# First-layer biases of the expert units applied by ScalarE from columns, low parts formed on GpSimd

## The chip, the cores and the metric

The kernel runs on one core of a Trainium2 chip. The metric is the device time of one execution in microseconds (us). TensorE multiplies, VectorE and ScalarE work on tiles in SBUF and in the matmul accumulator (PSUM), GpSimd works on SBUF, and SyncE issues most DMAs. Each engine runs its own list of instructions in order and waits on semaphores for the others.

## What the reference computes

The input x is 16 batches of 128 tokens with 256 features. Four stages are added to it in turn:

```
x = x + attention(layernorm(x), ctx, mask)              # one masked attention
x = x + experts(layernorm(x))                           # 2 of 4 encoder layers for each batch
x = x + causal_attention(layernorm(x), ctx)             # 16 heads
x = x + shared_ffn_and_top1_of_8(layernorm(x))

# one encoder layer (expert e):
x1 = layernorm(x + attention_16_heads(x)) * n1w + n1b
ff = relu(x1 @ l1w.T + l1b) @ l2w.T + l2b               # 256 -> 1024 -> 256
out = layernorm(x1 + ff) * n2w + n2b
```

The change touches `l1b`, the biases of the first layer inside `relu`, in the second stage.

## The kernel before

A **unit** is one batch with one of its two chosen experts: 32 units, one batch being units 2b and 2b+1. The stage is written as a fully unrolled list of blocks, n = -1 to 32, and each engine has its own function `block` that gives its order within a block. Block n works on four units at once: unit m = n+1 gets its scores, unit n its attention values and output projection, unit f = n-1 its first layer norm and hidden layer, unit g = n-2 its second layer, and unit n-3 its second layer norm. In even blocks the next batch is also prepared (`kp` is not None there): normalised tokens are transposed and split. In odd blocks its statistics are taken. Blocks 31 and 32 do this too for the causal stage that follows.

Every float32 product is made from bf16 parts: a high part and a low part (value minus high part), with three matmuls per product.

What the order is on each engine in block n (names are the functions of the kernel, lines are those of the profile):

- **TensorE**: `projection_v(m)`; `second(g,1)`; `values(n)` (L716); `x1_transposes(f)` (L492, reads x1, waits for `x1_ready(f)`); `second(g,0)`; `o_rows(n)`; `scores(m)`; in even blocks `prep`; `hidden(f,1)` (L752 to L756); `o_transposes(n)`; `hidden(f,0)`; `shift_transpose(m)` (L679, waits for VectorE's maxima of the scores); `out_proj(n)` (L498 to L500, waits for VectorE's `o_low(n)`); `projection_qk` of the next unit (L632 to L642, waits for `yT_ready`, which `y_low` gives in even blocks); `scores_T(m)`.
- **ScalarE**: `exps(n)`, `qk_hi(m)`, `o_evict(n)`, `x1_hi(f)`, in even blocks `prep`, `relu(f,1)` (L1149), `oo(n)`, `shift(m)`, `relu(f,0)`.
- **VectorE**: `norm1(f)`, `bias_v(m)`, `add_expert(n-4)`, in even blocks `y_of`, then `qk_low(m)`, `x1_low(f)`, `sum2(g)`, `o_norm(n)`, `maxima(m)`, `shift_split(m)`, `o_low(n)` (L1542), `norm2(n-3)` (L1288, waits for GpSimd's root `l2_rstd`), in even blocks `y_low` (L1502), `h_low(f,1)` (L1569), `sum1(n)` and its statistics, `h_low(f,0)`, statistics of g, in odd blocks statistics of the next batch.
- **GpSimd**: `rstd(1)` for unit f (L1980, L1982), in even blocks `y_root`, `y_bias(m)` (L2054), `affine1(f)` (L2064, L2066, which gives `x1_ready(f)`), `x1_bias(f)` (L2073), `rstd(2)` for unit n-3, `affine2(n-3)` (L2077, L2079, waits for `norm2(n-3)`).

In `hidden` each of the eight 128-column slices of the hidden layer starts with a product of the bias row (split into high and low rows in `b1hl`) with a row selector, and then takes six weight products. `relu` reads PSUM once (128x512) and writes the high part `hh`; `h_low` reads PSUM again and writes the low part `hl`. `second` multiplies both with the second layer's weights.

Of the kernel before, what the change touches and what calls it, by code (L numbers as in the profile page):

```python
# [80 lines left out]
B_QK = DFF  # L81
B_ALL = DFF + 2 * D
# [43 lines left out]
def encoder_kernel(nc, x_d, ctx_d, mask_d, maskt_d, w_d, wc_d, vec_d, vc_d, b1_d, gw_d, gb_d, sw_d, sv_d, tw_d, tvec_d, tg_d, tb_d,  # L126
# [8 lines left out]
    with stack:  # L135
# [10 lines left out]
        b1hl = sb("b1hl", [128, B_ALL], bf16)  # L146
        cst = sb("cst", [128, C_ALL])
# [57 lines left out]
        kraw = vec[:, 0:K_ALL]  # L205
        gl = h[:, 0:12 * B * E].rearrange("p (k j) -> p k j", j=B * E)
# [27 lines left out]
        def sem(name):  # L234
# [18 lines left out]
                                    "gveps", "grstd", "g", "gm", "gmean"))  # L253
        mask_ready, neg_ready, g_sums, g_centred = a_m01, a_neg, a_sm, a_sn
# [72 lines left out]
        def head(g, c, s):  # L327
            return 8 * c + 2 * g + s

        b1f = [(0, 512, v[0:NROW, :, :].rearrange("p h k -> p (h k)")), (512, 512, qk[0:NROW, :]),  # L330
               (B_QK, D, khm[0:NROW, :, :, :].rearrange("p c s k -> p (c s k)").bitcast(f32)),
# [23 lines left out]
        def _(sp):  # L355
# [16 lines left out]
            for c0, width, rows_f in b1f:  # L372
                sp.dma_start(rows_f, b1_d[:, c0:c0 + width]).then_inc(b1_in, 16)
            sp.dma_start(s12_raw, sw_d[:, 0:KC * 2 * HM]).then_inc(sw_in, 16)
# [111 lines left out]
        def _(pe):  # L486
# [253 lines left out]
            def hidden(u, half, base, e):  # L740

                if half == 1:
                    pe.wait_ge(x1T_split, u + 1)
                elif not isinstance(u, int) or u > 0:
                    pe.wait_ge(res2, u)

                def w(t, c, j):
                    return t[:, ds(base + (W_L1 + 512 * half + 128 * j + c * DFF), 128)]
                for j in range(4):
                    b0 = 512 * half + 128 * j  # L750
                    dst = ps[:, 7 - half, 128 * j:128 * j + 128]
                    mm(dst, b1hl[:, b0:b0 + 128], row_of(e), start=True, stop=False)  # L752
                    for c in range(KC):
                        mm(dst, w(w_hi, c, j), xh[:, c, :], start=False, stop=False)  # L754
                        mm(dst, w(w_hi, c, j), xl[:, c, :], start=False, stop=False)  # L755
                        last = mm(dst, w(w_lo, c, j), xh[:, c, :], start=False, stop=(c == KC - 1))  # L756
                last.then_inc(h_b if half else h_a, 1)

            def second(u, half, base):

                if half == 1:
                    pe.wait_ge(hl_b, u + 1)
                    pe.wait_ge(hl_a, u + 1)
# [161 lines left out]
            pe.wait_ge(b1_ready, 4)  # L925
# [102 lines left out]
        def _(act):  # L1028
# [47 lines left out]
            for i in range(PAIRS):  # L1076
# [14 lines left out]
                if i == 2:  # L1091
                    act.wait_ge(b1_zero, 1)
                    act.wait_ge(b1_in, 16 * 4)
# [53 lines left out]
            def relu(u, half):  # L1147
                act.wait_ge(h_b if half else h_a, u + 1)
                A(hh[:, 4 * half:4 * half + 4, :], ps[:, 7 - half, :].rearrange("p (c k) -> p c k", k=128),  # L1149
                  ACT.Relu).then_inc(hh_b if half else hh_a, 1)  # L1150

            def block(n, kp):
# [9 lines left out]
                if kp is not None:  # L1162
                    prep(kp, 2 * KC if isinstance(kp, int) and kp >= B else KC)
                if encodes(f):
                    relu(f, 1)
                if attends(n):
                    oo(n)
# [107 lines left out]
        def _(dve):  # L1275
# [106 lines left out]
            for i in range(PAIRS):  # L1382
# [11 lines left out]
                if i + 2 < PAIRS:  # L1394
                    if i == 0:
                        dve.wait_ge(x_third, 16)
                    if i == 1:
                        dve.wait_ge(x_in2, 16)
# [8 lines left out]
                if i == 4:  # L1407
                    dve.wait_ge(b1_ready, 4)
# [158 lines left out]
            def h_low(u, half):  # L1567
                dve.wait_ge(hh_b if half else hh_a, u + 1)
                stt(hl[:, 4 * half:4 * half + 4, :], ps[:, 7 - half, :].rearrange("p (c k) -> p c k", k=128), 0.0,  # L1569
                    hh[:, 4 * half:4 * half + 4, :], ALU.max, ALU.subtract).then_inc(hl_b if half else hl_a, 1)  # L1570

# [88 lines left out]
            def block(n, slot, bias_m, add_b, ks, kp):  # L1660
# [28 lines left out]
                if encodes(f):  # L1689
                    h_low(f, 1)  # L1690
# [6 lines left out]
                if encodes(f):  # L1697
                    h_low(f, 0)
# [128 lines left out]
            dve.wait_ge(sv_in, 32)  # L1827
            for b in range(1, B):
# [145 lines left out]
        def _(pool):  # L1974
# [92 lines left out]

            def x1_bias(u, slot, base):
# [12 lines left out]
            def block(n, slot, ex, kp, km):  # L2081

                m, f = n + 1, n - 1
                if encodes(f):
                    rstd(1, n, l1_var, l1_veps, l1_rstd)
                if kp is not None:
# [30 lines left out]
            def block_c(b, slot, ex=None, weights=False, tokens=False):  # L2117
                n = b + UNITS
                if served(b - 1):
                    rstd(1, b + (A1 - 1), s_var, s_veps, s_rstd)  # L2120
                if served(b + 1):
# [28 lines left out]
            def base_of(u):  # L2150
                return digit(words_pool[u // WORD], u % WORD) * V_EXP
            for n in range(-1, UNITS + 1):
# [132 lines left out]
```

## Time and profile before

| what | value |
|---|---|
| median of 3 runs | 782.21 us (781.33 to 782.88) |
| the profiled execution's own time | 782.31 us |
| its span, first to last instruction | 780.5 us |
| TensorE busy | 716.6 us (92%) |
| VectorE busy | 620.0 us (79%) |
| GpSimd busy | 378.5 us (48%) |
| ScalarE busy | 338.8 us (43%) |
| mean granted TensorE clock | 0.962 of full speed |

Busy time is an average over stages with different limits: the expert units run from about 100 us to 550 us of the span. TensorE's clock has two levels, 2.4 GHz (1.00) and 1.2 GHz (0.50). A row of the timeline gives the start, the duration, the engine, the line, what is written from what, and in brackets how long the engine had been idle and what ended the wait. A row of a stretch gives its length and the busy time and instructions of TensorE's matmuls, its weight loads, VectorE, ScalarE and GpSimd, then the mean granted clock, the DMA share and GB/s.

### The profile page before, as it was taken

What the parts mean: (1) busy time and instruction counts of PE and PEld (TensorE: products, weight loads), DVE (VectorE), ACT (ScalarE), POOL (GpSimd) and SP (SyncE); (2) the same over time, 40 slices, a digit from 0 to 9 for tenths busy, and PEclk for the clock granted to TensorE, in tenths of its full rate; (3) what the DMA queues carried; (4) which work ended last, traced back from release to release, by engine and by line L of the source; (5) the groups of instructions that cost most, each with busy time, mean ns of one, the idle gap of its engine ahead of it and who ended that gap; (6) DMA issues with size and microseconds to landing.
All of it is one profiled execution on the core that took longest, in us unless ns stands there. A gap on an engine that the chain in (4) does not pass through costs nothing.

```text
span 780.5 us, 29149 instructions
## 1 busy us (share of the span) xinstructions
PE 716.6 (92%) x11014; PEld 567.3 (73%) x11014; DVE 620.0 (79%) x1803; ACT 338.8 (43%) x711; POOL 378.5 (48%) x637
## 2 busy tenths in 40 slices
PE   5687879999999999999999999999999999987896
PEld 4466557888888888888888888888666566665684
DVE  4686665878888878888797878788889988997864
ACT  4676224343434344343434343434455555553210
POOL 4688523353535354544545353534434554547354
PEclk9797689999999999999999999999999999999798
DMA  9787200000000000000000000000112232322120
GB/s 313 253 266 274 89 2 3 3 3 3 3 3 4 3 3 3 3 3 3 3 3 4 3 3 3 3 16 10 43 57 81 78 90 90 104 89 69 38 73 7
DMA packets 24799, 40.98 MB, mean 53 GB/s; under 512 B 3871, under 2 KB 16809, under 8 KB 24411
## 3 DMA queue, kind: packets, MB, share of 16 engines
q1 hardware_dynamic: 23240, 37.13, 14.3%
q8 instruction: 96, 1.57, 0.8%
q0 software_dynamic: 704, 1.71, 0.8%
q10 hardware_dynamic: 726, 0.30, 0.2%
q14 instruction: 33, 0.27, 0.1%
HBM read 30.60 MB, written 8.91 MB: 51 GB/s over the span
## 4 chain that ended last, share of the span: by engine, by line
PE 69%; DVE 13%; POOL 5%; issue 4%; DMA 4%; ACT 4%; POOLq 0%; SPq 0%; ACTq 0%; DVEq 0%
PE ps L498 7%; PE ps L492 7%; PE ps L500 6%; PE ps L499 6%; PE ps L698 6%; DVE mx L1522 4%; PE ps L640 4%; PE ps L716 4%; PE ps L754 4%; PE ps L756 3%; PE ps L755 3%; DMA stage<-in_w 3%; PE ps L642 3%; PE ps L641 2%; PE ps L752 2%
## 5 line engine op out<-in xcount | busy, mean ns | idle before, releaser
L1131 ACT ACTIVATE pT<-ps 128x1024 f32<-128x1024 f32 x96 | 93.1, 1021 | 123.2 <-PE ps L698 123.2
L1522 DVE TENSOR_REDUCE mx<-ps 128x16 f32<-128x2048 f32 x48 | 109.5, 2281 | 1.0 <-PE ps L659 1.0
L2077 POOL TENSOR_TENSOR y<-y,vec 128x256 f32<-128x256 f32 x32 | 23.2, 726 | 171.3 <-DVE y L1288 171.3
L754 PE MATMUL ps<-xh,w_hi 128*128 128x128 bf16 x512 | 99.4, 219 | 0.0
L755 PE MATMUL ps<-xl,w_hi 128*128 128x128 bf16 x512 | 99.3, 219 | 0.0
L756 PE MATMUL ps<-xh,w_lo 128*128 128x128 bf16 x512 | 99.3, 219 | 0.0
L1982 POOL TENSOR_TENSOR rs<-rs,cst 128x1 f32<-128x1 f32 x132 | 75.6, 573 | 10.3
L1980 POOL TENSOR_TENSOR rs<-mv,cst 128x1 f32<-128x1 f32 x132 | 28.0, 212 | 99.7 <-DVE mv L1285 93.1
L498 PE MATMUL ps<-w_hi,hh 128*128 x256 | 69.8, 273 | 0.0
L499 PE MATMUL ps<-w_hi,hl 128*128 x256 | 69.8, 273 | 0.0
L500 PE MATMUL ps<-w_lo,hh 128*128 x256 | 69.8, 273 | 0.0
L1149 ACT ACTIVATE hh<-ps 128x512 bf16<-128x512 f32 x64 | 38.4, 600 | 67.8 <-PE ps L756 67.8
L640 PE MATMUL ps<-ycT_hi,w_hi 128*128 128x128 bf16 x256 | 58.9, 230 | 0.2
L641 PE MATMUL ps<-ycT_lo,w_hi 128*128 128x128 bf16 x256 | 56.8, 222 | 0.0
L642 PE MATMUL ps<-ycT_hi,w_lo 128*128 128x128 bf16 x256 | 56.7, 222 | 0.0
L752 PE MATMUL ps<-kst,b1hl 128*128 x256 | 56.2, 220 | 0.1
L754 PEld LDWEIGHTS ps<-xh,w_hi 128*128 x512 | 50.1, 98 | 1.2 <-issue 0.2
L2014 POOL TENSOR_TENSOR w_lo<-stage,w_hi 128x384 bf16<-128x384 f32 x48 | 45.4, 978 | 10.9 <-ACT w_hi L1032 10.9
L755 PEld LDWEIGHTS ps<-xl,w_hi 128*128 x512 | 50.1, 98 | 0.0
L756 PEld LDWEIGHTS ps<-xh,w_lo 128*128 x512 | 50.1, 98 | 0.0
L632 PE MATMUL ps<-kst,b1hl 128*128 (+1 forms) x192 | 42.7, 222 | 1.8 <-issue 0.6
L698 PE MATMUL ps<-qh,khm 32*128 32x128 bf16 x768 | 43.6, 217 | 0.4 <-ACT mT L1032 0.4
(361 smaller groups left out, 2436.1 us busy)
## 6 DMA issues: line engine op xcount, KB each, us to landing
stage<-in_w SPq DMA_DIRECT2D x32, 384.0 KB, 4.9
vec<-in_vec SPq DMA_DIRECT2D x4, 896.0 KB, 5.7
vec<-in_tw SPq DMA_DIRECT2D x12, 256.0 KB, 2.9
ctxc<-in_ctx SPq DMA_DIRECT2D x19, 128.0 KB, 2.2
comb<-x SPq DMA_DIRECT2D x16, 128.0 KB, 1.7
comb<-x1b SPq DMA_DIRECT2D x16, 128.0 KB
out<-x SPq DMA_DIRECT2D x16, 128.0 KB, 2.1
ytok<-t SPq DMA_DIRECT2D x14, 128.0 KB, 1.8
```

Source lines behind the costliest of these rows:

```text
L498: mm(dst, lhs_hi(j), rhs_hi(j), start=(first and j == 0), stop=False)
L499: mm(dst, lhs_lo(j), rhs_hi(j), start=False, stop=False)
L500: last = mm(dst, lhs_hi(j), rhs_lo(j), start=False, stop=(final and j == chunks - 1))
L640: mm(dst, w1, ycT_hi[:, src, :], start=False, stop=False)
L642: last = mm(dst, w2, ycT_hi[:, src, :], start=False, stop=(c == KC - 1))
L698: last = mm(att[:, g, 2 * c + s, :], lhs, rhs, start=(not causal and k == 0), stop=stop)
L754: mm(dst, w(w_hi, c, j), xh[:, c, :], start=False, stop=False)
L755: mm(dst, w(w_hi, c, j), xl[:, c, :], start=False, stop=False)
L756: last = mm(dst, w(w_lo, c, j), xh[:, c, :], start=False, stop=(c == KC - 1))
L1131: A(pT[:, 8 * a:8 * a + 8, :].rearrange("p h q -> p (h q)"), ps[:, 2 * a:2 * a + 2, :].rearrange("p g k -> p (g k)"), ACT.Exp, scale=SCALE ...
L1522: nc.vector.tensor_reduce(mx[:, :], att.rearrange("p g s k -> p (g s) k"), AX.X, ALU.max, negate=True).then_inc(m_max, 1)
L1982: tt(rs[:, i, :], rs[:, i, :], halves, ALU.pow).then_inc(done, 1)
```

## The change

The bias of the first layer is no longer multiplied in by TensorE. It is loaded as columns (`bcols`), eight columns for each expert; GpSimd copies a unit's eight columns into a ring of four slots (`bunit`), and ScalarE's `relu` adds a column to each 128-column slice. A column differs between slices, so `relu` is now four activations for each half, which write float32 (`hf`), and one more copy that makes the high part `hh` from it. The low part is `hf` minus `hh`; both lie in SBUF, and GpSimd computes it instead of VectorE. On GpSimd `h_low(n-2,0)` stands behind the first root of the block, and `h_low(f,1)` behind `x1_bias(f)` and ahead of `rstd(2)` and `affine2(n-3)`. On ScalarE `oo(n)` now stands ahead of `relu(f,1)`. The start of the kernel loads and splits two bias row pieces instead of four.

```diff
@@ TensorE, hidden
-                    b0 = 512 * half + 128 * j
                     dst = ps[:, 7 - half, 128 * j:128 * j + 128]
-                    mm(dst, b1hl[:, b0:b0 + 128], row_of(e), start=True, stop=False)
                     for c in range(KC):
-                        mm(dst, w(w_hi, c, j), xh[:, c, :], start=False, stop=False)
+                        mm(dst, w(w_hi, c, j), xh[:, c, :], start=(c == 0), stop=False)
@@ TensorE, second
                 if half == 1:
                     pe.wait_ge(hl_b, u + 1)
+                    pe.wait_ge(hh_a, u + 1)
+                else:
                     pe.wait_ge(hl_a, u + 1)
@@ ScalarE
             def relu(u, half):
                 act.wait_ge(h_b if half else h_a, u + 1)
-                A(hh[:, 4 * half:4 * half + 4, :], ps[:, 7 - half, :].rearrange("p (c k) -> p c k", k=128),
-                  ACT.Relu).then_inc(hh_b if half else hh_a, 1)
+                act.wait_ge(bunit_ready, 1 + u + 1)
+                if u > 0:
+                    act.wait_ge(hl_b if half else hl_a, u)
+                for j in range(4):
+                    k = 4 * half + j
+                    last = A(hf[half][:, 128 * j:128 * j + 128], ps[:, 7 - half, 128 * j:128 * j + 128], ACT.Relu,
+                             bias=bunit[:, u % RING, k:k + 1])
+                last.then_inc(hf_ready, 1)
+                act.wait_ge(hf_ready, 16 + u * 2 + (1 if half else 2))
+                copy(hh[:, 4 * half:4 * half + 4, :], hf[half].rearrange("p (c k) -> p c k", k=128)).then_inc(hh_b if half else hh_a, 1)
@@ ScalarE, block
+                if attends(n):
+                    oo(n)
                 if encodes(f):
                     relu(f, 1)
-                if attends(n):
-                    oo(n)
@@ VectorE, block
-                if encodes(f):
-                    h_low(f, 1)
...
-                if encodes(f):
-                    h_low(f, 0)
@@ GpSimd
+            def h_low(u, half):
+                pool.wait_ge(hh_b if half else hh_a, u + 1)
+                tt(hl[:, 4 * half:4 * half + 4, :], hf[half].rearrange("p (c k) -> p c k", k=128),
+                   hh[:, 4 * half:4 * half + 4, :], ALU.subtract).then_inc(hl_b if half else hl_a, 1)
+
+            def unit_bias(u):
+
+                cols = bcols[:, ds(digit(words_pool[u // WORD], u % WORD) * B_COLS, B_COLS)]
+                nc.gpsimd.tensor_copy(bunit[:, u % RING, :], cols).then_inc(bunit_ready, 1)
@@ GpSimd, block
                 if encodes(f):
                     rstd(1, n, l1_var, l1_veps, l1_rstd)
+                if encodes(n - 2):
+                    h_low(n - 2, 0)
                 if kp is not None:
                     y_root(kp)
...
                 if encodes(f):
                     affine1(f, ex(-1))
                     x1_bias(f, 1 - slot, ex(-1))
+                if encodes(f):
+                    h_low(f, 1)
                 if encodes(n - 3):
                     rstd(2, n - 2, l2_var, l2_veps, l2_rstd)
                     affine2(n - 3, ex(-3))
+                if encodes(n + 2):
+                    unit_bias(n + 2)
@@ SyncE, at the start
+            sp.dma_start(bcols[:, :], bc_d).then_inc(bcols_in, 16)
```

## Rows read from the trace of the kernel before

**Rows 1.** The page, part 1: busy time, share of the span, instructions.

```profile
PE 716.6 (92%) x11014; PEld 567.3 (73%) x11014; DVE 620.0 (79%) x1803; ACT 338.8 (43%) x711; POOL 378.5 (48%) x637
```

**Rows 2.** Timeline of TensorE in the units.

```profile
300.79 0.23 PE L632 MATMUL ps<-kst,b1hl 128*128 x1
...
307.09 0.33 PE L492 MATMUL ps<-cst,x 128*128 128x128 f32 x1
...
312.85 0.22 PE L756 MATMUL ps<-xh,w_lo 128*128 128x128 bf16 x1
312.90 0.22 PE L679 MATMUL ps<-identb,mtile 128*128 128x128 bf16 x1
...
313.19 0.28 PE L498 MATMUL ps<-w_hi,ooh 128*128 x1
...
320.32 0.41 PE L492 MATMUL ps<-cst,x 128*128 128x128 f32 x2
```

**Rows 3.** Timeline of VectorE in the units.

```profile
299.71 0.40 DVE L1288 TENSOR_SCALAR y<-t,mv,rs 128x256 f32<-128x256 f32 x1
300.03 0.42 DVE L1502 TENSOR_TENSOR ycT_lo<-ps,ycT_hi 128x256 bf16<-128x256 f32 x1
...
312.64 0.42 DVE L1542 TENSOR_TENSOR ool<-ps,ooh 128x256 bf16<-128x256 f32 x1
```

**Rows 4.** Timeline of ScalarE: first half's relu in three blocks (even, odd, even).

```profile
298.32 0.60 ACT L1149 ACTIVATE hh<-ps 128x512 bf16<-128x512 f32 x1 [1.19 <-PE ps L756]
...
311.31 0.60 ACT L1149 ACTIVATE hh<-ps 128x512 bf16<-128x512 f32 x1 [3.22 <-PE ps L756]
...
324.78 0.60 ACT L1149 ACTIVATE hh<-ps 128x512 bf16<-128x512 f32 x1 [1.19 <-PE ps L756]
```

**Rows 5.** Timeline of GpSimd, from odd block to even block.

```profile
313.56 0.73 POOL L2077 TENSOR_TENSOR y<-y,vec 128x256 f32<-128x256 f32 x1 [6.25 <-DVE y L1288]
314.46 0.73 POOL L2079 TENSOR_TENSOR y<-y,vec 128x256 f32<-128x256 f32 x1 [0.18 <-POOL y L2077]
315.25 0.19 POOL L1980 TENSOR_TENSOR rs<-mv,cst 128x1 f32<-128x1 f32 x1
315.52 0.55 POOL L1982 TENSOR_TENSOR rs<-rs,cst 128x1 f32<-128x1 f32 x1
316.96 0.31 POOL L1980 TENSOR_TENSOR rs<-mv,cst 128x1 f32<-128x1 f32 x1 [0.89 <-DVE mv L1285]
...
317.86 0.72 POOL L2054 TENSOR_TENSOR ybo<-y,vec 128x256 f32<-128x256 f32 x1
318.54 0.73 POOL L2064 TENSOR_TENSOR x<-x,vec 128x256 f32<-128x256 f32 x1
319.44 0.73 POOL L2066 TENSOR_TENSOR x<-x,vec 128x256 f32<-128x256 f32 x1 [0.17 <-POOL x L2064]
```

**Rows 6.** Groups by line: shapes, count, busy us and mean ns, idle before.

```profile
L752 PE MATMUL ps<-kst,b1hl 128*128 x256 | 56.2, 220 | 0.1
L1569 DVE SCALAR_TENSOR_TENSOR hl<-ps,hh 128x512 bf16<-128x512 f32 x64 | 42.9, 671 | 0.0
L2101 POOL TENSOR_TENSOR w_lo<-vec,w_hi 128x512 bf16<-128x512 f32 x12 | 13.9, 1161 | 0.0
L1056 ACT ACTIVATE t<-ps,mx 128x128 f32<-128x128 f32 x8 | 2.9, 362 | 0.0
L1032 ACT CAST vec<-vec 128x512 bf16<-128x512 f32 x1 | 0.6, 602 | 0.0
```

**Rows 7.** Groups by line, forms apart: a bias row piece at the start.

```profile
L1032 ACT CAST b1hl<-v 5x512 bf16<-5x512 f32 x1 | 0.6, 612 | 0.0
```

**Rows 8.** Timeline of TensorE; two stretches: busy times, then granted clock, DMA.

```profile
111.95 0.29 PE L679 MATMUL ps<-identb,mtile 128*128 128x128 bf16 x1 [2.25 <-DVE mtile L1530]
...
111.00:117.00 6.00, 4.92 (x47) 4.17 (x51) 3.33 (x11) 0.27 (x1) 1.53 (x4) 0.50 0.01 3
...
770.00:773.00 3.00, 3.00 (x15) 1.92 (x14) 1.07 (x3) 0.00 (x0) 0.99 (x1) 0.53 0.02 5
```

More of the change, by code:

```diff
@@ L80 @@
 K_ALL = K_ROW + NROW
-B_QK = DFF
-B_ALL = DFF + 2 * D
+B_QK = 0
+B_ALL = 2 * D
+B_COLS = FC
+RING = 4
 def batch_of(u):
@@ L123, in served, with encoder_kernel @@
     return not isinstance(b, int) or 0 <= b < B
-def encoder_kernel(nc, x_d, ctx_d, mask_d, maskt_d, w_d, wc_d, vec_d, vc_d, b1_d, gw_d, gb_d, sw_d, sv_d, tw_d, tvec_d, tg_d, tb_d,
+def encoder_kernel(nc, x_d, ctx_d, mask_d, maskt_d, w_d, wc_d, vec_d, vc_d, b1_d, bc_d, gw_d, gb_d, sw_d, sv_d, tw_d, tvec_d, tg_d, tb_d,
                    ib_d, it_d, cst_d, kst_d, pos_d, out, comb_d, ytok_d, keys_d):
@@ L146, in encoder_kernel @@
         b1hl = sb("b1hl", [128, B_ALL], bf16)
+        bcols = sb("bcols", [128, E * B_COLS])
+        bunit = sb("bunit", [128, RING, B_COLS])
+        hf_a = sb("hf_a", [128, 512])
         cst = sb("cst", [128, C_ALL])
@@ L205, in encoder_kernel @@
         kraw = vec[:, 0:K_ALL]
+        hf = (hf_a, h[:, 512:1024])
         gl = h[:, 0:12 * B * E].rearrange("p (k j) -> p k j", j=B * E)
@@ L253, in encoder_kernel @@
                                     "gveps", "grstd", "g", "gm", "gmean"))
+        bcols_in, hf_ready, bunit_ready = x_in2, x_in1, b1_zero
         mask_ready, neg_ready, g_sums, g_centred = a_m01, a_neg, a_sm, a_sn
@@ L328, in head @@
             return 8 * c + 2 * g + s
-        b1f = [(0, 512, v[0:NROW, :, :].rearrange("p h k -> p (h k)")), (512, 512, qk[0:NROW, :]),
-               (B_QK, D, khm[0:NROW, :, :, :].rearrange("p c s k -> p (c s k)").bitcast(f32)),
+        b1f = [(B_QK, D, khm[0:NROW, :, :, :].rearrange("p c s k -> p (c s k)").bitcast(f32)),
                (B_QK + D, D, klm[0:NROW, :, :, :].rearrange("p c s k -> p (c s k)").bitcast(f32))]
@@ L924, in _ @@
             pe.wait_ge(w_hi_ready, PAIRS * 4)
-            pe.wait_ge(b1_ready, 4)
+            pe.wait_ge(b1_ready, 2)
             pe.wait_ge(vones_ready, 4)
@@ L1092, in _ @@
                     act.wait_ge(b1_zero, 1)
-                    act.wait_ge(b1_in, 16 * 4)
+                    act.wait_ge(b1_in, 16 * 2)
                     for c0, width, rows_f in b1f:
@@ L1397, in _ @@
                     if i == 1:
-                        dve.wait_ge(x_in2, 16)
+                        dve.wait_ge(x_in2, 32)
                     pair_stats(i + 2)
@@ L1407, in _ @@
                 if i == 4:
-                    dve.wait_ge(b1_ready, 4)
+                    dve.wait_ge(b1_ready, 2)
                     for slot in range(2):
@@ L1565, in x1_low @@
                    ALU.subtract).then_inc(x1T_split, 1)
[L1567 to L1570, printed above, removed]
             def sum2(u, slot):
@@ L1827, in _ @@
             dve.wait_ge(sv_in, 32)
+            dve.wait_ge(hl_b, UNITS)
             for b in range(1, B):
@@ L2120, in block_c @@
                     rstd(1, b + (A1 - 1), s_var, s_veps, s_rstd)
+                if b == 1:
+                    h_low(UNITS - 1, 0)
                 if served(b + 1):
@@ L2151, in base_of @@
                 return digit(words_pool[u // WORD], u % WORD) * V_EXP
+            pool.wait_ge(bcols_in, 32)
+            unit_bias(0)
             for n in range(-1, UNITS + 1):
@@ L2253 @@
     vc = cat([at["bv"], at["bo"], f1["s_ln_g"], f1["s_ln_b"]])[None, :]
-    b1 = cat([cat([f0["lin1_b"], f0["in_proj_b"][:, :2 * D]], axis=1),
-              cat([np.zeros(DFF, np.float32), at["bq"], at["bk"]])[None, :]])
+    b1 = cat([f0["in_proj_b"][:, :2 * D], cat([at["bq"], at["bk"]])[None, :]])
+    bc = f0["lin1_b"].reshape(E * B_COLS, 128).T
     e12 = cat([cat([f1["ew1"][e], f1["ew2"][e]]).T for e in range(EM)], axis=1)
@@ L2268 @@
         "maskt": a["mask_Bx1xS2_ik1"].reshape(B, S).T,
-        "w": w, "wc": wc, "vec": vec, "vc": vc, "b1": b1,
+        "w": w, "wc": wc, "vec": vec, "vc": vc, "b1": b1, "bc": bc,
         "gw": f0["gate_w"].T.reshape(KC, 128, E).transpose(1, 0, 2), "gb": f0["gate_b"][None, :],
```

## The prediction

> **What bounds the kernel now.** I read the page first: TensorE is busy 92% of the span, VectorE 79%, GpSimd 48%, ScalarE 43% [rows 1]. Next the timeline of the units, engine by engine, since there the change acts. The reader is to see in the TensorE rows that matmuls follow each other at 0.05 to 0.06 us, and that the next wait is already near: the transpose of the maxima starts at 312.90, but out_proj only at 313.19 [rows 2], because VectorE's o_low runs from 312.64 to 313.06 [rows 3]. Last the GpSimd rows, which show a chain that ends almost on TensorE's path. norm2 comes in at 313.56, then follow affine2, the root of unit f, y_root, y_bias and affine1, which ends at 320.17 [rows 5]; x1_transposes starts at 320.32 [rows 2], 0.15 later. In the odd-to-even step GpSimd has nothing to spare. GpSimd idles 6.25 us before affine2 [rows 5], but its place in the order matters, not its load.
>
> One block lasts 12.99 us (298.32 to 311.31, even to odd) or 13.47 us (311.31 to 324.78, odd to even) [rows 4]; 26.5 us a pair.
>
> **The change part by part.**
>
> TensorE: 8 matmuls a unit go, 256 in all [rows 6], at a pitch of 0.056 us: 0.45 us a unit, 14.3 us in all. They stand in hidden, beside VectorE's chain of maxima, split and o_low. Removing 0.45 us there brings TensorE earlier to out_proj, where in the odd block it already waits for VectorE. So even alone this part would yield little. What I use below is 0.22 us for the half that ends before relu(f,1).
>
> ScalarE: relu(f,1) was one operation of 0.60 us [rows 4]. A bias from a column at 128 elements is not there for relu; the nearest row is an exp with such a bias, 0.362 us [rows 6], overlapping the next by 0.10, as other ScalarE rows do: 3 x 0.26 + 0.36 = 1.14 us. Bounds: 0.60 (the pieces cost what one did) and 1.45 (no overlap). I take 1.14, the same form. Then 0.1 for waiting for its own result, and the copy, 0.60 [rows 6]. The Trainium skill, "ScalarE: Activation LUTs", section "What ACT_TABLE_LOAD costs", gives 280 ns plus 0.833 ns an element with a pointer bias and 93 ns of overlap: by it, as an estimate, four pieces take 1.27 us instead of 1.14. The row is used. The copy reads SBUF and its row has the same shape. The added waits of relu, for the unit's columns and for the low part of the unit before, are met early: unit_bias runs two blocks ahead, and the low parts are done a block before (their price if not: relu would move by the lateness, one for one). ScalarE itself has cover: it idled 3.22 us before relu in the odd block [rows 4]. The second half's extra 1.2 us lies ahead of the next exps, where projection_qk and scores_T (3.3 us of TensorE) cover it. shift(m) now stands behind a longer relu(f,1), but its result is only needed after projection_qk, 2.2 us later.
>
> VectorE: both h_low go, 2 x 0.67 us a unit [rows 6]. That brings the root of the next unit and the batch statistics up to 1.3 us forward: 0.89 us of GpSimd's idle time before y_root [rows 5] could go, the largest gain that I see in it. But VectorE first has to get past norm2, see below.
>
> GpSimd: two h_low a unit. The same form, two inputs of 128x512 into bf16, takes 1.16 us [rows 6]. Bounds: 0.73 (one of 256 columns) and 1.46 (twice that) [rows 5]. I take 1.16. The Trainium skill, "GPSIMD Engine Reference", section "Engine selection", says that two-input elementwise work belongs on VectorE and is about 2x slower on GpSimd; the rows give 1.16 against 0.67, 1.7x. By the page, an estimate of 2 x 0.67 = 1.34, each block would be 0.36 longer than in the sum below. unit_bias copies 8 columns: between 0.19 (one column) and 0.73 (256) [rows 5]; I take 0.25.
>
> The step that decides is the new place. On GpSimd h_low(f,1) waits for ScalarE's high part of this block, and behind it are queued rstd(2) and affine2 of unit n-3, then the next block's root, h_low(.,0), y_root, y_bias and affine1. On VectorE norm2(n-3) waits for rstd(2), and behind norm2 are queued y_low, sum1, all statistics, norm1 and bias_v. I add it up from T, the moment ScalarE sees the end of hidden(f,1):
>
> - oo first, to 0.5; four pieces to 1.66; own result and copy to 2.36
> - GpSimd h_low from 2.46 to 3.62; rstd(2), 0.82 [rows 5], to 4.4
> - 0.17 to VectorE; norm2, 0.40 [rows 3], from 4.6 to 5.0 (before it ran right behind o_low)
> - 0.19 to GpSimd; affine2, 1.63 (313.56 to 315.19) [rows 5], to 6.8; unit_bias to 7.05
> - root of unit n 0.82 to 7.85; h_low(.,0) 1.16 to 9.0; y_root 0.90 to 9.9; y_bias 0.68 to 10.6; affine1 1.63 to 12.2; x1_transposes at 12.35.
>
> From x1_transposes to the next T TensorE works without a stop: 320.32 to 324.78 is 4.46, less 0.22 is 4.24 [rows 2, 4]. Odd to even is then 12.35 + 4.24 = 16.6 us, before 13.47: +3.1. TensorE would be ready for x1_transposes near 8.7 (320.2 - 311.3 - 0.22) and stands 3.5 us.
>
> Even to odd there is no y_root: 11.45. But y_low follows norm2, from 4.92 to 5.34, and projection_qk waits for it until 5.45 (before, 300.79 - 298.32 = 2.5); from there to x1_transposes it took 6.30 (300.79 to 307.09) [rows 2]. So 11.75, plus 4.22 - 0.22 = 4.0, is 15.75, before 12.99: +2.75.
>
> A pair gains some 5.8 us. The whole chain needs norm2, so it holds from block 3 to 32: 29 steps x 2.9 = 84 us. The same delay shows once more where the causal blocks take over, +3. At the start two of four bias pieces go, 0.61 us on ScalarE each with overlap [rows 7], and as much on VectorE beside it: -1. The new load of 16 KB takes the place of two small ones and costs nothing; if it did, statistics of the later batches would wait for it. Sum: +86 on the profiled execution's 782.3, which is 0.1 from the median: 868 us.
>
> **The clock.** At 111.95 TensorE came out of a wait of 2.25 us, and over 111 to 117 us the granted clock was 0.50 (1.2 GHz) [rows 8]. The 4.92 us busy there [rows 8] would have been some 2.5 us at 2.4 GHz. Each pair now has a wait of 3.5 us and one near 2.8 us (2.69 to 5.45), both longer. Work behind them is TensorE's alone, so what the clock costs is not hidden. One fall a pair of 2.3 us (between 1.5, half of the 3 us at 0.53 from 770 to 773 us, and 3.0, half of 6 us from 111 to 117 [rows 8]): 15 x 2.3 = 34 us, 902 us. Two falls a pair: 935. The Trainium skill, "TensorE: Matmul & The Clock Gate", section "HAM oscillation — how this bites in real kernels", says that idle gaps between bursts bring the engine back to its lower clock again and again. By that rule the falls come every time; the trace agrees in the one gap of such length.
>
> **The rivals.**
>
> 1. The queue chain without falls of the clock: 868. For it: before these waits TensorE is dense, while the stretch before 110 us was sparse. Against it: the waits are longer.
> 2. Faster: GpSimd's chain is covered after all and the 256 matmuls are on the path: 782.3 - 14.3 = 768. It is decided where affine1 ends: before 8.7 us behind T. My sum says 12.2, so 3.5 us would have to be wrong. For it: 52% idle GpSimd. Against it: the order, in which every link is a semaphore.
> 3. No change: the chain is covered, but TensorE's 0.45 us only lengthens its wait for o_low (313.19 behind 313.06 [rows 2, 3]): 780 to 782.
>
> **How the numbers follow.** The measurement tells 0.2%, 1.6 us, from no change. Chances: chain with falls 0.60, chain without 0.27, faster 0.05, no change 0.03, something between (steps of half my length, about 820 us) 0.05. Predicted is the likeliest, 902. Bounds of the unknown costs: relu pieces -0.54 or +0.3 and two h_low -0.86 or +0.6 a step, over 29 steps -41 or +26; not all at once. 868 less half of the lower one is 848; two falls a pair give 935, rounded to 940. Faster 0.05, same 0.03, slower 0.92.
>
> **What would show it.** In the changed profile: norm2 (L1288 on y from t or h) no longer behind o_low but waiting for GpSimd's root; x1_transposes waiting about 3.5 us for POOL x in odd-to-even steps; projection_qk waiting for ycT_lo in even blocks; a pair of 32 to 37 us; TensorE busy below 85%; granted clock under 0.95 in the units. The prediction is wrong if x1_transposes waits under 1 us, or if the clock in the units stays 1.00 (then 868).

## The result, and the profile after

The changed kernel takes 893.94 us (median of 4 runs, 893.75 to 895.58); the kernel before takes 782.08 us (781.33 to 782.88). The ratio is 1.1435, with a 95% interval of 1.1415 to 1.1455. That is 112 us slower. The forecast was 902 us, in a range of 848 to 940, and the rival without falls of the clock was 868.

The page of the changed kernel, part 1 (busy time, share of the span, instructions), and the line of the granted clock from part 2:

```profile
span 892.2 us, 29016 instructions
...
PE 744.7 (83%) x10758; PEld 584.5 (66%) x10758; DVE 605.3 (68%) x1737; ACT 410.8 (46%) x965; POOL 450.6 (51%) x733
...
PEclk9797889898898998998988988988999999999798
```

Against [rows 1], TensorE has 256 matmuls fewer and yet is busy 28 us longer, while its share falls from 92% to 83%. Both are signs of other costs than work: matmuls at half clock take longer, and there are new waits. The engines that got work are far from full, GpSimd at 51%, ScalarE at 46%. The busy shares alone would not name the bound.

The chain that ended last, by engine:

```profile
PE 44%; POOL 20%; DVE 14%; ACT 9%; issue 8%; DMA 4%; POOLq 1%; ACTq 0%; SPq 0%; DVEq 0%
```

In the kernel before this chain was 69% TensorE and 5% GpSimd. Now a fifth of the time that sets the end lies on GpSimd, which is busy half of the time. The waits say where (what waited, for what: total us, times, longest):

```profile
PE ps L639 <- DVE ycT_lo L1517: 44.4, 16, 3.2
...
PE ps L499 <- POOL x L2073: 37.3, 15, 2.9
```

```profile
POOL hl L2077 <- ACT hh L1039: 231.6, 32, 9.2
...
DVE y L1303 <- POOL rs L1989: 78.9, 32, 3.1
```

TensorE waits once in each pair of blocks before x1_transposes (L499) and once before projection_qk (L639), 82 us in all. Behind both stands one chain: GpSimd's h_low of the first half waits for ScalarE's copy, norm2 waits for the root that stands behind it on GpSimd, and the rest follows. It is read best in one step, here from an even to an odd block. The times are start and length; in brackets stands the wait before. ScalarE first, then GpSimd, VectorE and TensorE:

```profile
338.09 0.37 ACT L1039 CAST ooh<-ps 128x256 bf16<-128x256 f32 x1 [1.19 <-PE ps L499]
338.36 1.15 ACT L1161 ACTIVATE h<-ps,bunit 128x128 f32<-128x128 f32 x4
339.54 0.62 ACT L1039 CAST hh<-h 128x512 bf16<-128x512 f32 x1
```

```profile
340.23 1.15 POOL L2077 TENSOR_TENSOR hl<-h,hh 128x512 bf16<-128x512 f32 x1 [7.52 <-ACT hh L1039]
341.34 0.19 POOL L1987 TENSOR_TENSOR rs<-mv,cst 128x1 f32<-128x1 f32 x1
341.61 0.55 POOL L1989 TENSOR_TENSOR rs<-rs,cst 128x1 f32<-128x1 f32 x1
342.79 0.73 POOL L2094 TENSOR_TENSOR y<-y,vec 128x256 f32<-128x256 f32 x1 [0.63 <-DVE y L1303]
...
344.36 0.19 POOL L2083 COPY bunit<-bcols 128x8 f32 x1
...
345.30 1.15 POOL L2077 TENSOR_TENSOR hl<-hf_a,hh 128x512 bf16<-128x512 f32 x1
```

```profile
339.14 0.42 DVE L1557 TENSOR_TENSOR ool<-ps,ooh 128x256 bf16<-128x256 f32 x1
342.20 0.41 DVE L1303 TENSOR_SCALAR y<-t,mv,rs 128x256 f32<-128x256 f32 x1 [2.64 <-POOL rs L1989]
342.52 0.42 DVE L1517 TENSOR_TENSOR ycT_lo<-ps,ycT_hi 128x256 bf16<-128x256 f32 x1
```

```profile
343.29 0.29 PE L639 MATMUL ps<-kst,b1hl 128*128 x1 [2.76 <-DVE ycT_lo L1517]
...
367.76 0.41 PE L499 MATMUL ps<-cst,x 128*128 128x128 f32 x2 [2.86 <-POOL x L2073]
```

In the kernel before, norm2 begins 0.33 us after o_low begins (its o_low stands in [rows 3], at 312.64):

```profile
312.97 0.40 DVE L1288 TENSOR_SCALAR y<-h,mv,rs 128x256 f32<-128x256 f32 x1
```

Here o_low begins at 339.14 and norm2 at 342.20, because the root on GpSimd could not begin before h_low had left the queue. In the kernel before, norm2 ran right behind o_low, so the root's own input is there in time; here GpSimd idled 7.52 us before h_low, with the root queued behind it. y_low follows norm2, and TensorE comes to projection_qk 2.76 us late. The wait before x1_transposes is the same lateness one step later: it starts in the odd block and goes through norm2, affine2, the next root, h_low of the second half, y_root, y_bias and affine1 into the next even block (the chain of [rows 5], with two h_low in it).

Then the clock. Stretches of the same step: busy times and counts, then granted clock, share of DMA, GB/s.

```profile
338.00:342.00 4.00, 2.40 (x32) 1.80 (x29) 1.49 (x4) 3.85 (x12) 1.69 (x3) 1.00 0.01 2
342.00:343.00 1.00, 0.00 (x0) 0.00 (x0) 0.80 (x3) 0.02 (x1) 0.37 (x2) 0.64 0.00 0
343.00:349.00 6.00, 5.71 (x96) 5.08 (x97) 3.88 (x12) 0.65 (x1) 5.39 (x10) 0.50 0.01 3
350.00:365.00 15.00, 14.71 (x265) 11.88 (x262) 10.09 (x31) 8.98 (x24) 5.84 (x11) 1.00 0.01 2
```

At the end of the wait the granted clock goes from 1.00 to 0.50 (2.4 to 1.2 GHz) and stays there for the first 6 us of TensorE's work, then comes back. In the kernel before it was 1.00 from 118 us to the end of the units.

The steps from one first-half relu to the next, read off ScalarE's timeline as in [rows 4]: 16.1 to 16.5 us odd to even (before 13.5 to 13.7; one step with a fall took 18.02), 15.78 in the one even-to-odd step where no fall came, and 17.9 to 18.1 in the twelve with one (before 13.0 to 13.2). So falls came in 13 of the 27 steps from block 3 up to the last two, all but one of them in the wait before projection_qk. The last two steps are 19.24 and 19.10 (before 14.64 and 14.77), and each has a fall too:

```profile
611.40:630.70 19.30, 16.22 (x238) 13.51 (x236) 11.56 (x32) 8.31 (x22) 8.68 (x14) 0.82 0.03 8
630.70:649.80 19.10, 15.92 (x241) 12.89 (x239) 11.33 (x31) 8.26 (x22) 8.69 (x14) 0.91 0.04 9
```

That is 15 falls in 29 steps. Over the 29 steps the relu of the last block moved from 540.65 to 649.75 us, 109 of the 112 us.

### The profile page after: what moved, and what is told of

The parts are those of the page before. It is cut to its first block, busy times and chain, and to the rows that moved or that the text cites. A ratio compares the mean times of both kernels' runs of the same rounds, so it can differ in the third digit from the quotient of the medians.

```text
span 892.2 us, 29016 instructions
## 1 busy us (share of the span) xinstructions
PE 744.7 (83%) x10758; PEld 584.5 (66%) x10758; DVE 605.3 (68%) x1737; ACT 410.8 (46%) x965; POOL 450.6 (51%) x733
## 4 chain that ended last, share of the span: by engine, by line
PE 44%; POOL 20%; DVE 14%; ACT 9%; issue 8%; DMA 4%; POOLq 1%; ACTq 0%; SPq 0%; DVEq 0%
PE ps L499 6%; POOL hl L2077 6%; PE ps L705 5%; PE ps L505 4%; DVE mx L1537 4%; ACT h L1161 4%; PE ps L507 4%; PE ps L506 4%; POOL rs L1989 4%; DMA stage<-in_w 3%; PE ps L647 2%; POOL w_lo L2021 2%; PE ps L649 2%; ACT hh L1039 2%; PE ps L648 2%
## 5 line engine op out<-in xcount | busy, mean ns | idle before, releaser
L2077 POOL TENSOR_TENSOR hl<-h,hh 128x512 bf16<-128x512 f32 x32 | 36.9, 1153 | 231.6 <-ACT hh L1039 231.6
L759 PE MATMUL ps<-xh,w_hi 128*128 128x128 bf16 x512 | 94.2, 221 | 0.2 <-DVE xl L1579 0.2
L761 PE MATMUL ps<-xh,w_lo 128*128 128x128 bf16 x512 | 93.5, 219 | 0.0
L760 PE MATMUL ps<-xl,w_hi 128*128 128x128 bf16 x512 | 93.4, 219 | 0.0
L639 PE MATMUL ps<-kst,b1hl 128*128 (+1 forms) x192 | 47.4, 247 | 44.8 <-DVE ycT_lo L1517 44.4
L647 PE MATMUL ps<-ycT_hi,w_hi 128*128 128x128 bf16 x256 | 66.8, 261 | 0.1
L648 PE MATMUL ps<-ycT_lo,w_hi 128*128 128x128 bf16 x256 | 65.9, 258 | 0.0
L649 PE MATMUL ps<-ycT_hi,w_lo 128*128 128x128 bf16 x256 | 65.9, 257 | 0.0
L639 PEld LDWEIGHTS ps<-kst,b1hl 128*128 128x128 bf16 x192 | 21.3, 111 | 54.4 <-issue 52.9
L1303 DVE TENSOR_SCALAR x<-t,mv,rs 128x256 f32<-128x256 f32 x32 | 39.0, 1219 | 21.2 <-POOL rs L1989 21.2
L1039 ACT CAST ooh<-ps 128x256 bf16<-128x256 f32 x48 | 17.9, 372 | 75.5 <-PE ps L499 75.5
```

What stands on the lines that cost most here:

```text
L647: mm(dst, w1, ycT_hi[:, src, :], start=False, stop=False)
L648: mm(dst, w1, ycT_lo[:, src, :], start=False, stop=False)
L759: mm(dst, w(w_hi, c, j), xh[:, c, :], start=(c == 0), stop=False)
L2077: tt(hl[:, 4 * half:4 * half + 4, :], hf[half].rearrange("p (c k) -> p c k", k=128), hh[:, 4 * half:4 * half + 4, :], ALU.subtract).then_i ...
```

## The experiments

All ratios are to the kernel before, run on the same chip. Its medians there were 781.3 to 781.8 us. "The changed kernel" is the one with the whole change.

**e1: h_low of the first half behind the root and affine2.**

```
                 if encodes(n - 3):
                     rstd(2, n - 2, l2_var, l2_veps, l2_rstd)
                     affine2(n - 3, ex(-3))
+                if encodes(f):
+                    h_low(f, 1)
```

(and the same two lines taken away above the root.)

> The changed kernel, with one move on GpSimd: h_low(f,1) stands behind rstd(2) and affine2(n-3). All work, its engine and its length are unchanged. Theory (the place in GpSimd's queue): norm2 runs right behind o_low again, from T+1.7, affine2 ends at T+3.9, h_low(f,1) at 5.0, and the rest of the chain is 6.0 root, 7.1 h_low(.,0), 8.0 y_root, 10.3 affine1, x1_transposes at 10.5: odd to even 14.7 us (changed kernel 16.2), even to odd 13.6 (17.9), no wait of projection_qk for ycT_lo, granted clock in the units 1.00; 782 + 29 x 0.85 = about 807 us. Rival (the amount of work, GpSimd's 1.15 us twice and ScalarE's longer relu, is what costs): nothing of that has changed, so near 890 us.

806.4 us (804.3 to 808.3), ratio 1.031 (1.0277 to 1.0342). One line's place in a queue is worth 87 us. The work is the same and stays on the same engines. Steps became 13.4 to 13.6 and 14.7 to 15.2 us, the clock in the units behind the first blocks 1.00. Of TensorE's two waits the one for y_low is gone and the other is left:

```profile
PE ps L499 <- POOL x L2073: 25.8, 27, 1.8
```

**e2: only the root ahead of h_low, affine2 behind it.**

```
+                if encodes(n - 3):
+                    rstd(2, n - 2, l2_var, l2_veps, l2_rstd)
                 if encodes(f):
                     h_low(f, 1)
                 if encodes(n - 3):
-                    rstd(2, n - 2, l2_var, l2_veps, l2_rstd)
                     affine2(n - 3, ex(-3))
```

> The changed kernel, with the root rstd(2) alone moved ahead of h_low(f,1); affine2 stays behind it. It frees VectorE's norm2 and what is queued behind it (y_low, sum1, statistics), but not GpSimd's own chain: h_low(f,1) still waits for ScalarE until T+2.4. Theory: if VectorE's wait is the larger part, even to odd falls to 13.9 us and odd to even to 15.0 us, about 814 us and close to the run with h_low(f,1) behind affine2. Rival (GpSimd's own chain behind ScalarE's high part is the larger part, VectorE's wait only rides along): little better than the changed kernel, 870 to 890 us.

809.34 us (806.15 to 809.68), ratio 1.0345 (1.0308 to 1.0382), steps 13.6 to 13.8 and 14.6 to 15.0, but 17.31 in the last but one, in which the clock fell once. Norm2's wait for the root was the harm to VectorE and to projection_qk. What affine2 adds behind h_low is small: 3 us against e1, part of it that one fall.

**e3: both h_low on VectorE, at their places of before, reading hf and hh.**

```
@@ VectorE
+            def h_low(u, half):
+                dve.wait_ge(hh_b if half else hh_a, u + 1)
+                tt(hl[...half...], hf[half]..., hh[...half...], ALU.subtract)...
...
                     y_low(kp[0], ...)
+                if encodes(f):
+                    h_low(f, 1)
...
@@ GpSimd: h_low and its three calls taken out
```

> The changed kernel with both h_low back on VectorE at their old places, reading the float32 value and the high part from SBUF. Bias columns and the longer relu on ScalarE stay, bias products stay out. Theory: VectorE takes up h_low(f,1) at T+2.4 instead of T+2.0, the statistics behind it are 0.4 us late, and half of the 0.45 us of TensorE comes back ahead of relu: odd to even 13.65, even to odd 12.95 us, 782 us, plus or minus 4, clock 1.00. Rival (ScalarE's relu of 1.15 us with its copy is the main cost): two thirds of the loss stay, 850 us or more.

789.18 us (787.87 to 791.88), ratio 1.011 (1.0075 to 1.0144). Steps are 13.0 to 13.2 us and mostly 14.05, where 13.65 had been expected for the second. That is the miss: 0.4 us in 15 steps, 6 us. The rest of the wait stands before x1_transposes, in the odd-to-even steps only:

```profile
PE ps L499 <- POOL x L2082: 9.6, 16, 1.1
```

Two operations of that step are longer than in the kernel before. h_low of the second half takes 0.87 us (0.66 before, when it read PSUM) beside a GpSimd copy that itself takes 0.66 and not 0.19; the first operation of affine1 takes 0.92 us (0.73 in [rows 5]) beside one of VectorE. The first delays the statistics that y_root waits for, the second lies on the chain itself; together they are the 0.4 us:

```profile
318.20 0.87 DVE L1584 TENSOR_TENSOR hl<-hf_a,hh 128x512 bf16<-128x512 f32 x1
321.48 0.72 DVE L1604 SCALAR_TENSOR_TENSOR x<-y,gate_w,x 128x256 f32<-128x256 f32 x1
```

```profile
318.46 0.66 POOL L2087 COPY bunit<-bcols 128x8 f32 x1
321.87 0.92 POOL L2080 TENSOR_TENSOR x<-x,vec 128x256 f32<-128x256 f32 x1
```

So with relu in pieces and the products gone, but h_low on VectorE, about 8 us are lost; the place on GpSimd brings the other 104.

**e4: TensorE's two waits filled.** Into each of the two waits of a pair, in even blocks from 4 to 30 (before projection_qk to 28), go 12 matmuls of 512 columns into a free PSUM bank. Nothing reads them.

```
+            def fill(bank, count):
+                for _ in range(count):
+                    mm(ps[:, bank, :], identb[:, :], ...4 x 128 columns of identb, start=True, stop=True)
...
+                    if isinstance(n, int) and 4 <= n <= UNITS - 2 and n % 2 == 0:
+                        fill(1, 12)
                     x1_transposes(f)
...
+                    if 4 <= n < UNITS - 3 and n % 2 == 0:
+                        fill(1, 12)
                     projection_qk(next_k, base, e)
```

> The changed kernel with 12 extra matmuls of 512 columns (2.6 us, written to a free bank and never read) ahead of x1_transposes and ahead of projection_qk in the even blocks 4 to 30, that is inside TensorE's two long waits. They take no time from anything if they fit in the waits of 2.8 us. Theory (the half clock costs 2.1 us in nearly every pair): granted clock 1.00 in the units, even to odd 15.8 instead of 17.9 us, 894 - 13 x 2.1 = 866 us. Rival (the clock's falls cost nothing, the step of 17.9 us is another wait): 894 us or more, with the step unchanged.

866.63 us (860.66 to 869.3), ratio 1.108 (1.1019 to 1.1141). TensorE does over 300 matmuls more and the kernel is 27 us faster than the changed one. Steps were 15.6 to 15.8 and 16.0 to 16.8. The two 50-us stretches (busy times, then clock):

```profile
250.00:300.00 50.00, 48.20 (x725) 36.45 (x724) 33.84 (x90) 24.93 (x64) 27.32 (x44) 1.00 0.01 2
300.00:350.00 50.00, 48.59 (x750) 36.91 (x751) 34.55 (x89) 24.22 (x60) 26.53 (x45) 1.00 0.01 3
```

The same stretches of the changed kernel:

```profile
250.00:300.00 50.00, 41.21 (x678) 33.94 (x677) 34.27 (x91) 23.65 (x59) 25.78 (x43) 0.93 0.01 2
300.00:350.00 50.00, 41.11 (x641) 33.74 (x639) 31.86 (x81) 22.07 (x55) 25.64 (x42) 0.90 0.01 2
```

With the waits of the chain left as they are and the clock at 1.00, 27 us go. That is the least that the clock costs: some odd-to-even steps are up to 0.6 us longer with the filling, and one fall was left, in the last step but one (17.91 us), where the wait before projection_qk was not filled. Read off the steps of the changed kernel the falls cost more, 32 us. The 12 with 17.9 to 18.1 against 15.78 make 26, the one of 18.02 against 16.2 makes 1.8. The two of the last steps make 3.7: in e10 below, which fills nothing there either, the last two steps had no fall and took 17.21 and 17.46 us. So the clock's share of the 112 us is 27 to 32, the chain's 80 to 85. The clock of e10 over its last two steps:

```profile
594.48:611.69 17.21, 13.59 (x237) 11.22 (x235) 12.11 (x32) 8.35 (x21) 8.89 (x14) 1.00 0.03 10
611.69:629.15 17.46, 14.38 (x241) 11.57 (x239) 11.64 (x31) 8.26 (x21) 8.70 (x14) 1.00 0.03 10
```

**e5: the kernel before without its 256 bias products** (the first layer's biases are left out, nothing applies them).

```
-                    mm(dst, b1hl[:, b0:b0 + 128], row_of(e), start=True, stop=False)
                     for c in range(KC):
-                        mm(dst, w(w_hi, c, j), xh[:, c, :], start=False, stop=False)
+                        mm(dst, w(w_hi, c, j), xh[:, c, :], start=(c == 0), stop=False)
```

> The kernel before without its 256 first-layer bias products and nothing else changed; the first layer's biases are left out of the result. It prices what the change takes off TensorE. Theory (VectorE's chain of maxima, split and o_low already sets out_proj in the odd block): 0 to 0.22 us a unit come back, 775 to 781 us. Rival (TensorE's matmuls are all on the path): 14.3 us less, 767 us.

781.44 us (778.52 to 782.96, 12 runs), ratio 0.9999 (0.9984 to 1.0014). The steps stay as they were, 12.9 to 13.2 and 13.4 to 13.8 us. TensorE's timeline at the end of hidden, and VectorE's o_low:

```profile
312.55 0.23 PE L679 MATMUL ps<-identb,mtile 128*128 128x128 bf16 x1
312.97 0.28 PE L498 MATMUL ps<-w_hi,ooh 128*128 x1 [0.19 <-DVE ool L1541]
```

```profile
312.41 0.42 DVE L1541 TENSOR_TENSOR ool<-ps,ooh 128x256 bf16<-128x256 f32 x1
```

In [rows 2] out_proj began 0.29 us after that transpose, now 0.42. In both kernels it begins 0.13 to 0.14 us behind the end of o_low (313.06 and 312.83). TensorE comes to the place sooner and waits there for o_low, which is VectorE's. The saving that the change was built on doesn't exist in this kernel: the products lay beside the chain of VectorE.

**e6: e3 with two moves in the order.** On GpSimd affine1 goes ahead of y_bias. On VectorE qk_low goes ahead of y_of.

```
@@ VectorE
+                qk_low(m)
                 if kp is not None:
                     y_of(...)
-                qk_low(m)
@@ GpSimd
                     y_root(kp)
+                if encodes(f):
+                    affine1(f, ex(-1))
                 if causal(m):
...
                 if encodes(f):
-                    affine1(f, ex(-1))
                     x1_bias(f, 1 - slot, ex(-1))
```

> The run with the low parts on VectorE, with two moves more: on GpSimd y_bias stands behind affine1 (x1_transposes no longer waits for it, 0.68 us), on VectorE y_of stands behind qk_low, so that it is not held by the later y_bias. The run it builds on has odd-to-even steps of 14.05 us with TensorE waiting up to 1.1 us for x1. Theory (its excess over before is that wait): steps of 13.3 to 13.5 us, 789 - 16 x 0.6 = 779 us, a little under the kernel before. Rival (ScalarE's longer relu limits it elsewhere): no better than 789 us.

779.73 us (776.09 to 780.78, 12 runs), ratio 0.9968 (0.9951 to 0.9985). TensorE's waits for POOL x are down from 9.6 to 0.4 us.

**e7: the kernel before with the same two moves**, as the control.

> The kernel before with the same two moves (y_bias behind affine1 on GpSimd, y_of behind qk_low on VectorE) and nothing of the change. TensorE waited 0.1 us for x1 in the odd-to-even steps there, so 0 to -2 us: 779 to 782 us. It is the control for the run with low parts on VectorE and these moves.

779.65 us (776.43 to 781.11, 12 runs), ratio 0.9972 (0.9958 to 0.9986). So the 0.3% of e6 is all the order's. With the moves, biases from columns are worth as much as biases by products, within the 0.2% that these runs can tell.

**e8: e7 without the 256 products** (the first layer's biases left out again).

> The kernel before with both moves and without the 256 bias products (first-layer biases left out of the result). The most that any way of removing them can give in this order of work. Theory: TensorE gets 0.22 to 0.45 us a unit until it meets VectorE's o_low: 772 to 777 us. Rival (all matmuls on the path): 767 us or less.

779.86 us (775.91 to 781.78, 12 runs), ratio 0.9967 (0.9951 to 0.9983). This was expected to gain and didn't. Even with the chain of GpSimd out of the way, the products cost nothing. TensorE's waits for POOL x are down to 0.2 us in this run, and the meeting with o_low is still there:

```profile
PE ps L498 <- DVE ool L1541: 3.5, 15, 0.9
```

**e9: the part on GpSimd alone.** relu is one operation of 0.60 us again, into f32, and a bias product stands in each slice (with one bias row for all, so that the biases differ from the reference's).

```
+                    mm(dst, b1hl[:, 0:128], row_of(e), start=True, stop=False)
...
-                for j in range(4):
-                    k = 4 * half + j
-                    last = A(hf[half][:, 128 * j:...], ps[:, 7 - half, ...], ACT.Relu, bias=bunit[...])
+                last = A(hf[half][:, 0:512], ps[:, 7 - half, :], ACT.Relu)
```

> The GpSimd part of the change alone: both h_low on GpSimd at the places of the changed kernel, while relu is one ScalarE operation again (float32 out, then the copy) and TensorE has a bias product for each slice again. The product takes other bias rows than the first layer's, so the biases in the result are not the right ones; the work is the same. Theory (GpSimd's place in the queue is the cause): relu is 0.55 us shorter, hidden 0.22 us longer, so 0.33 us less a step: 894 - 29 x 0.33 = 884 us, clock about 0.91. Rival (the bias part on ScalarE is the main cause): under 830 us.

885.31 us (884.49 to 885.67), ratio 1.1321 (1.1298 to 1.1343). The relu that is shorter by 0.55 us brings back only 9 us, as expected. Steps are 16.6 to 16.8 even to odd (17.9 to 18.1 in the changed kernel) and 17.3 to 17.6 odd to even (there 16.1 to 16.5). The two steps without a fall took 15.75 odd to even and 15.58 even to odd, which is the shorter relu. In the other pairs the clock now falls behind both waits, each time for about half as long as in the changed kernel. In one pair TensorE came out of them at 161.61 and 172.60 us:

```profile
163.00:166.00 3.00, 3.00 (x22) 2.06 (x21) 1.65 (x4) 0.09 (x1) 0.00 (x0) 0.50 0.00 0
166.00:172.00 6.00, 4.09 (x64) 3.75 (x62) 3.09 (x6) 3.15 (x7) 1.85 (x3) 1.00 0.01 3
173.00:176.00 3.00, 3.00 (x42) 2.81 (x44) 1.93 (x7) 0.00 (x0) 2.92 (x6) 0.50 0.00 0
```

**e10 and e11: only one of the two waits filled.** e10 leaves out the filling before x1_transposes, e11 the one before projection_qk.

> The changed kernel with the 12 extra matmuls ahead of projection_qk alone; the wait before x1_transposes stays bare. In the changed kernel's trace the clock falls in the wait before projection_qk in nearly every pair. Theory A (a fall belongs to the wait it stands in): the falls are gone, 866 us, as with both waits filled. Theory B (either wait is enough for a fall): it moves to the wait before x1_transposes, odd-to-even steps become 18 us, and the time stays at 885 to 895 us.

875.66 us (871.76 to 877.13), ratio 1.1207 (1.1188 to 1.1226). Even to odd is 15.6 to 15.8 us, with no falls. Odd to even is 17.6 to 17.9 in 9 of 14 steps and 16.1 to 16.6 in the others. The wait before x1_transposes, behind which the clock had fallen once in the changed kernel, now has the falls. The second theory had said so; what it missed is that they are fewer and shorter, so that 875.66 is 9 us under its 885 to 895. One such step of e10 (x1_transposes at 325, after a wait of 2.76 us):

```profile
322.00:325.00 3.00, 0.58 (x22) 0.31 (x14) 2.66 (x8) 1.05 (x3) 2.75 (x5) 1.00 0.00 0
325.00:332.00 7.00, 6.66 (x70) 5.55 (x71) 4.29 (x7) 1.42 (x5) 0.92 (x2) 0.76 0.00 0
```

> The changed kernel with the 12 extra matmuls ahead of x1_transposes alone (even blocks); the wait before projection_qk stays bare. Both theories expect the falls there to stay: even-to-odd 17.9 us, 890 to 896 us. If the time drops to 866 us, what dropped the clock was the two waits together.

883.02 us (878.96 to 885.29), ratio 1.1292 (1.1253 to 1.1331). Steps are 16.0 to 16.8 odd to even and mostly 16.6 to 17.4 even to odd, later 17.95. The gain of 11 us was not expected of this wait, behind which the clock had fallen once. The steps say that most of the falls behind the other wait became shorter, and one stayed away (15.72).

**e12: e1 with the two moves of e6.**

> h_low(f,1) behind affine2 on GpSimd, as in the first experiment, and with y_bias behind affine1 and y_of behind qk_low: the best order found for low parts on GpSimd. It takes y_bias's 0.68 us off the chain that ends in x1_transposes: odd-to-even 14.8 - 0.68 = 14.1 us, even-to-odd 13.6 - 0.5 = 13.1 us, 806 - 14.5 x 0.68 - 14.5 x 0.5 = 789 us. If the chain's arithmetic is right this still is above the kernel before, since h_low's 2 x 1.15 us stay in it. Rival: GpSimd's load no longer matters once ordered, 780 us.

789.3 us (785.35 to 791.29), ratio 1.009 (1.0054 to 1.0125), steps 13.1 and 14.05. What is left of TensorE's wait for GpSimd:

```profile
PE ps L499 <- POOL x L2073: 9.0, 16, 0.9
```

With h_low on GpSimd in the best place that was tried, the kernel is still 7 us slower than the kernel before and 10 slower than e6.

## Why the prediction was right, point by point

**What bounds the kernel.** Right: the GpSimd chain of [rows 5] had nothing to spare, and the order, not the load, decided. e1 shows it most plainly, 87 us for the place of one call.

**TensorE's 256 products, worth almost nothing.** Right, and shown by e5 and e8: 0.9999 of before, and 779.86 against 779.65 with the order mended. The 0.22 us that the sum gave back a step is another matter. From x1_transposes to the next T the changed kernel took 4.23 us (4.24 in the sum), against 4.46 before: there TensorE works behind GpSimd's chain without a stop, and fewer products do show. In the kernel before and in e5, o_low sets the step and they don't.

**ScalarE's pieces.** Forecast 1.14 us from overlapping rows of 0.36 us; measured 1.15. The copy took 0.62 (forecast 0.60), and the wait for its own result 0.03 (forecast 0.1). By the Trainium skill, "ScalarE: Activation LUTs", section "What ACT_TABLE_LOAD costs", the estimate was 1.27; here the nearest row of the trace was the better guide.

**GpSimd's h_low.** Forecast 1.16 us, measured 1.153 over 32, against 0.671 on VectorE [rows 6], 1.7 times. unit_bias took 0.19 (forecast 0.25).

**The chain from T.** T is the moment ScalarE sees the end of hidden(f,1). In the kernel before, relu began at 298.32, 0.26 us behind the start of the last matmul of that half (298.06). In the changed kernel these matmuls are

```profile
337.61 0.22 PE L761 MATMUL ps<-xh,w_lo 128*128 128x128 bf16 x1
...
355.49 0.22 PE L761 MATMUL ps<-xh,w_lo 128*128 128x128 bf16 x1
```

so T is 337.87 in the even block shown and 355.75 in the odd one behind it. oo began 0.22 us later than T, since it also waits for o_transposes, but relu then began at T + 0.49, as forecast (0.5). Norm2 was put at T + 4.6 and came at 4.33. projection_qk was put at 5.45 and came at 5.42: norm2 and y_low were early, but it began 0.35 us behind the end of y_low and not 0.11. x1_transposes was put at 12.35 and came at 12.01. The third of a microsecond went in small terms: 0.09 in relu's pieces and the copy's gap, 0.04 us from the root to norm2 and not 0.17, and less in the short copies and roots; affine1 took 1.80 and not 1.63. TensorE's wait there was 2.86 us, forecast 3.5, for it was ready at T + 9.15 and not at 8.7; the wait before projection_qk was 2.76, forecast 2.8.

**The steps.** Even to odd without a fall: 15.78, forecast 15.75. Odd to even: 16.1 to 16.5, forecast 16.6. In the even-to-odd step without a fall (T = 304.07) projection_qk came at T + 5.57, x1_transposes 6.21 us later and the next T 4.00 us behind that (forecast 5.45, 6.30 and 4.00), so that this sum is right in its terms too. e1 and e2 show that norm2's wait for the root carries the even-to-odd step; in e3 and e12, where that root no longer waits for h_low, some 0.55 us of lateness are left in the odd-to-even step (14.05 against 13.5).

**Blocks 3 to 32, 29 steps, tail.** The delay did begin in block 3 (the step to 167.68 us, 16.33 long, is the first late one). The sum without falls was 868. e4, with the clock held at 1.00 in all units but the last, gave 866.6, and that it came so close is in part luck, since the filling costs something itself. With the falls taken out of its own steps the changed kernel is at 862: the delay without them is 2.7 us a step in the mean and not 2.9, also in the last two steps (2.6 and 2.7 by e10); their excess of 4.6 and 4.3 us is that and a fall each. The start gave back 0.2 us and not 1, the tail took 2.6 and not 3.

**The clock.** One fall a pair of 2.3 us was forecast, 15 falls and 34 us in all. Measured were 15 falls in the 29 steps, 12 of them of 2.1 to 2.3 us (17.9 to 18.1 against 15.78) and the others of 1.6 to 2.0, 32 us; e4 says 27 at the least. Right in kind and in size. The 8 us between 902 and 894 are then mostly the steps of 2.7 us. The section "HAM oscillation — how this bites in real kernels" of "TensorE: Matmul & The Clock Gate" in the Trainium skill says that gaps between bursts bring the clock down again and again. The kernel before had more such gaps than the one at 111.95 that the prediction names: TensorE also came out of waits of 3.98, 3.38 and 2.63 us at 25.45, 36.84 and 62.72, and the granted clock was 0.50 behind each. The changed kernel agrees too, with 15 falls, but not in every one of its gaps: each pair had two waits of 2.8 us, and only one of them had the fall. That there would be one fall a pair was a choice between one and two, which the prediction gave no reason for, and which of the waits would have it, it did not say. e9, e10 and e11 show that the fall isn't tied to one place.

**The rivals.** Faster, 768, is refuted by e5: the products were not on the path. It and no change both fail by affine1's end: the chain reached x1_transposes 12.01 behind T, and 8.7 would have been needed. 868 without falls fails by the clock.

**What was not foreseen:** the root of the 0.3% in e6 and e7, which needs no part of the change, and how much of the cost of the change without GpSimd goes with it. That part cost 8 us (e3), and after the two moves none (e6 against e7). Nor was it foreseen that VectorE and GpSimd slow each other, which is where e3 missed its 782 us.

## What to carry to other kernels

Before work is moved to a half-idle engine, read what stands behind the new place in that engine's queue, and who waits for it; here one call ahead of a root of 0.8 us cost 87 us, some 30 of them by the clock. Before work is taken off the busiest engine, check that engine's next meeting with another one: at 92% busy, removing 256 matmuls gave nothing that could be measured. A new wait on TensorE has two prices, its length and the clock behind it, and only an experiment that fills the wait tells them apart.

## What the runs showed of the hardware that was not expected

**VectorE and GpSimd slow each other.** The groups of norm1 on VectorE (count, busy us, mean ns, idle before), of the kernel before:

```profile
L1288 DVE TENSOR_SCALAR x<-t,mv,rs 128x256 f32<-128x256 f32 x32 | 17.4, 544 | 0.9 <-POOL rs L1982 0.9
```

and of the changed one:

```profile
L1303 DVE TENSOR_SCALAR x<-t,mv,rs 128x256 f32<-128x256 f32 x32 | 39.0, 1219 | 21.2 <-POOL rs L1989 21.2
```

An operation of this form takes 0.40 us at norm2 (rows above) and 1.24 beside h_low on GpSimd, and the rows of one place show them start 0.06 us apart and end 0.14 apart (364.48 and 364.34):

```profile
363.24 1.24 DVE L1303 TENSOR_SCALAR x<-t,mv,rs 128x256 f32<-128x256 f32 x1 [0.60 <-POOL rs L1989]
```

```profile
363.18 1.16 POOL L2077 TENSOR_TENSOR hl<-hf_a,hh 128x512 bf16<-128x512 f32 x1
```

The Trainium skill, "Trainium Architecture — The Big Picture", section "What this means for kernel authors", calls the ports that the two share an exclusive lock. The trace agrees that norm1 doesn't end before h_low does. It ends 0.14 us later, less than its own 0.40, so that what exactly stood still for how long these rows don't say. e3 shows it in the other direction too: a GpSimd copy of 0.19 us takes 0.66 beside h_low on VectorE. norm1's delay was not on the path in the changed kernel: affine1, which needs it, stands behind y_bias and began 1.33 us after norm1's end, at 365.81.

**The length of a wait does not say whether the clock falls.** Two waits of 2.8 us, one with falls in nearly every pair and one almost without; with the first filled (e10), the second got them. It isn't the nearness of another wait alone either. In the changed kernel the wait with the falls began some 7 us after TensorE had come out of the other (374.7 behind 367.76), and the one without them some 22 us after (364.90 behind 343.29); but with the other wait filled the falls came in each (e10 and e11). What decides stays open.
